# A 32-row block solve on VectorE: the next row finished by one fused operation, the other rows by product and addition in turn, and semaphore waits where drains stood

## The reference, cut to what matters

```python
q = silu(causal_conv(h @ Wq)); k = silu(causal_conv(h @ Wk)); v = silu(causal_conv(h @ Wv))
...
def step(S, inp):                       # one token of one head
    S = S * exp(g)                      # decay
    delta = (v - k @ S) * beta
    S = S + outer(k, delta)
    return S, q @ S
...
o = rms_norm(o) * g_norm_weight
return x + (o * silu(h @ Wg)).reshape(...) @ Wo
```

## Time and profile before

| | |
|---|---|
| device time, median of three runs | 1336.97 us (1332.95 to 1341.53) |
| span of the profiled execution, first to last instruction | 1334.4 us |
| busy share of the span | PE 84%, DVE 58%, PEld 54%, ACT 49%, POOL 25% |
| DMA | 44.83 MB, mean 34 GB/s |
| the three block solves, from the first transpose's start to the last one's end | 545.66 to 574.60, 662.86 to 691.78, 781.13 to 809.80 us |

### The profile page before, as it was taken

How to read it: one execution, slowest core, us unless ns; L and a number is a source line. 1 busy time by engine, 2 the same in 40 slices (tenths; PEclk the granted TensorE clock), 3 DMA queues, 4 the chain that set the end, 5 groups by cost and what they waited for, 6 DMA issues and landing times. The chain is left out here.

```text
span 1334.4 us, 25691 instructions
## 1 busy us (share of the span) xinstructions
PE 1123.0 (84%) x9898; PEld 723.0 (54%) x9899; DVE 775.0 (58%) x1947; ACT 660.2 (49%) x1386; POOL 334.3 (25%) x321
## 2 busy tenths in 40 slices
PE   6998886687989977779769856978899988798998
PEld 3565564354656633357437625856444444475776
DVE  4565557685654587868786785556372465453111
ACT  2565344552542255867696653535756452345342
POOL 1333300134010046545483510230000034700000
PEclk9999897698999976879988985989899988899999
DMA  7000000200000000000000000080286710000000
GB/s 305 1 1 1 2 3 0 97 1 1 3 2 0 1 1 0 0 2 2 1 1 2 1 1 1 2 352 3 48 178 134 153 17 1 2 3 1 1 0 16
DMA packets 18329, 44.83 MB, mean 34 GB/s; under 512 B 4992, under 2 KB 8096, under 8 KB 17568
## 3 DMA queue, kind: packets, MB, share of 16 engines
q1 hardware_dynamic: 18208, 43.20, 11.3%
HBM read 42.41 MB, written 0.79 MB: 32 GB/s over the span
## 5 line engine op out<-in xcount | busy, mean ns | idle before, releaser
L943 ACT ACTIVATE L_xattn_pT<-banks 128x512 f32<-128x512 f32 x128 | 69.0, 598 | 87.8 <-PE banks L821 87.8
L220 POOL TENSOR_TENSOR norm_rstd<-norm_var,norm_power 128x4 f32<-128x4 f32 x24 | 24.4, 1019 | 330.0 <-DVE norm_var L213 330.0
L1004 DVE TENSOR_REDUCE L_xattn_top<-banks 128x4 f32<-128x512 f32 x128 | 79.5, 684 | 35.0 <-PE banks L789 35.0
L1639 DVE TENSOR_TENSOR L_ffn_a<-L_ffn_a,L_ffn_share 128x512 f32<-128x512 f32 x64 | 39.9, 686 | 60.9 <-DMA L_ffn_share<-L_ffn_shares 60.7
L1866 ACT ACTIVATE L_ffn_aT<-banks,L_ffn_shift 128x512 f32<-128x512 f32 x64 | 43.3, 687 | 58.9 <-PE banks L1818 57.3
L1553 PE MATMUL banks<-L_ffn_a,region_a 128*128 128x512 f32 x136 | 67.5, 601 | 5.0 <-DVE L_ffn_a L1639 5.0
L1879 DVE SCALAR_TENSOR_TENSOR x<-banks,L_ffn_combine,x 128x128 f32<-128x128 f32 x64 | 18.0, 344 | 88.7 <-PE banks L1829 88.7
L1544 PE MATMUL banks<-hT,region_a 128*128 128x512 f32 x136 | 69.1, 614 | 0.0
L1829 PEld LDWEIGHTS banks<-region_b,L_ffn_aT 128*128 128x128 f32 x512 | 59.4, 192 | 6.7 <-issue 6.7
L499 ACT ACTIVATE L_attn_p<-banks,L_attn_shift 128x129 f32<-128x129 f32 x128 | 45.4, 369 | 34.3 <-DVE L_attn_shift L552 34.3
L1829 PE MATMUL banks<-region_b,L_ffn_aT 128*128 128x128 f32 x512 | 59.6, 275 | 0.0
(11 more groups left out here) (549 smaller groups left out, 2900.0 us busy)
## 6 DMA issues: line engine op xcount, KB each, us to landing
L_ffn_share<-L_ffn_shares SPq DMA_DIRECT2D x32, 512.0 KB, 10.6
region_b<-in_L_ffn SPq DMA_DIRECT2D x1, 6216.0 KB, 29.9
region_a<-in_L_ffn SPq DMA_DIRECT2D x1, 4416.0 KB, 13.6
region_b<-in_L_attn SPq DMA_DIRECT2D x1, 3150.5 KB, 10.4
region_a<-in_L_ffn SPq DMA_DIRECT2D x1, 3080.5 KB, 16.4
region_b<-in_L_attn SPq DMA_DIRECT2D x1, 1633.5 KB, 8.7
region_b<-in_L_xattn SPq DMA_DIRECT2D x1, 835.0 KB, 7.4
w_tables<-in_tables SPq DMA_DIRECT2D x1, 832.0 KB, 11.7
```

Of the source, the lines that this page charges most:

```text
L943: nc.scalar.activation(pT[:, n % 2, 4 * i:4 * i + 4, :], rows_of(flip[i][:], 4), ACT.Exp, scale=scale).then_inc(exped, 1)
L1004: nc.vector.tensor_reduce(top[:, 32 * i:32 * i + 32:HD], rows_of(score[i][:], 4), X, ALU.max).then_inc(topped, 1)
L1639: nc.vector.tensor_tensor(a[:, k % AHEAD, :], a[:, k % AHEAD, :], share[:, batch % RING, j, :], ALU.mult).then_inc(weighed, 1)
```

## The change

Finished rows now go back into `blocks`, in SBUF, and `solve`, in PSUM, holds only the sums of rows that aren't finished. Step j makes three operations where it made two:

- the product, now for the rows from j+2 on, (30 - j) x j numbers, with both inputs in `blocks`;
- one `scalar_tensor_tensor`, which finishes row j+1: row j of `blocks` times the number at (j+1, j), plus row j+1 of `solve`, written into row j+1 of `blocks` (j numbers);
- the addition of the product to the rows from j+2 on of `solve`.

Products lie in two buffers in turn. The drains between these operations are gone, but for one in step 1 and one at the end; each operation instead waits at a semaphore for the one that it needs, which stands two places earlier in DVE's order. DVE copies only the first half of `blocks` into `solve`, and ACT the second half (`copy_rest`). The ones of the diagonal are set within step 2, in `blocks`. `lower_c` and AT's diagonal blocks are transposed from `blocks` instead of `solve`. Since `joined` lies over `blocks`, both `keep_join` now wait for the `place_upper` that reads the part that they overwrite, and ACT does both `keep_lower` ahead of both `keep_join`.

```diff
-    step_out = from_spare(256)
+    products = from_spare(2 * 256)
...
+            def copy_rest(hg):
+                act.wait_ge(blocks_taken, hg + 1)
+                act.wait_ge(r_ready, B * (hg + 1))
+                nc.scalar.activation(solve[:, NB // 2:NB, :], blocks[:, NB // 2:NB, :], ACT.Copy).then_inc(rest_copied, 1)
...
             def keep_join(hg, half):
                 act.wait_ge(join_made, 2 * hg + half + 1)
+                act.wait_ge(upper_ready, 4 * hg + 2)
...
                 keep_blocks(first + B - 1)
+                copy_rest(hg)
...
                 keep_lower(hg, 0)
+                keep_lower(hg, 1)
                 keep_join(hg, 0)
                 keep_join(hg, 1)
-                keep_lower(hg, 1)
...
                 nc.vector.transpose(blocks[:], blocks_in).then_inc(blocks_taken, 1)
                 dve.drain()
-                nc.vector.tensor_copy(solve, blocks[:])
+                nc.vector.tensor_copy(solve[:, 0:NB // 2, :], blocks[:, 0:NB // 2, :])
+                rows, rests = (NB - 2) * hg, (NB - 3) * hg
+                for j in range(1, NB - 1):
+                    rest = NB - 2 - j
+                    product = products[:, 256 * (j % 2):256 * (j % 2) + rest * j].rearrange("p (i c) -> p i c", c=j)
+                    if j >= 2:
+                        dve.wait_ge(row_done, rows + j - 1)
+                    if rest > 0:
+                        nc.vector.tensor_tensor(product, bc(blocks[:, j + 2:NB, j], 2, j), bc(blocks[:, j, 0:j], 1, rest),
+                                                ALU.mult).then_inc(product_made, 1)
+                    if j == 1:
+                        dve.drain()
+                        dve.wait_ge(rest_copied, hg + 1)
+                    else:
+                        dve.wait_ge(rest_done, rests + j - 1)
+                    nc.vector.scalar_tensor_tensor(blocks[:, j + 1, 0:j], blocks[:, j, 0:j], blocks[:, j + 1, j:j + 1],
+                                                   solve[:, j + 1, 0:j], ALU.mult, ALU.add).then_inc(row_done, 1)
+                    if rest > 0:
+                        dve.wait_ge(product_made, rests + j)
+                        nc.vector.tensor_tensor(solve[:, j + 2:NB, 0:j], solve[:, j + 2:NB, 0:j], product,
+                                                ALU.add).then_inc(rest_done, 1)
+                    if j == 2:
+                        nc.vector.memset(blocks[:].rearrange("p t s -> p (t s)")[:, 0:NB * NB:NB + 1], 1.0)
                 dve.drain()
-                nc.vector.memset(solve.rearrange("p t s -> p (t s)")[:, 0:NB * NB:NB + 1], 1.0)
-                dve.drain()
-                for j in range(1, NB - 1):
-                    rest = NB - 1 - j
-                    product = step_out[:, 0:rest * j].rearrange("p (i c) -> p i c", i=rest)
-                    nc.vector.tensor_tensor(product, bc(blocks[:, j + 1:NB, j], 2, j), bc(solve[:, j, 0:j], 1, rest), ALU.mult)
-                    dve.drain()
-                    nc.vector.tensor_tensor(solve[:, j + 1:NB, 0:j], solve[:, j + 1:NB, 0:j], product, ALU.add)
-                    dve.drain()
                 after(dve, lower_kept, 2 * hg)
-                nc.vector.transpose(lower_c, solve.rearrange("p t s -> p s t")).then_inc(lower_ready, 1)
+                nc.vector.transpose(lower_c, blocks[:].rearrange("p t s -> p s t")).then_inc(lower_ready, 1)

             def place_upper(b):
                 nc.vector.transpose(AT[BLOCKS[b], :, :, BLOCKS[b]].rearrange("p b h t -> p t (b h)"),
-                                    solve[BLOCKS[b], :, :]).then_inc(upper_ready, 1)
+                                    blocks[BLOCKS[b], :, :]).then_inc(upper_ready, 1)

             def keep_join(hg, half):
                 dve.wait_ge(join_made, 2 * hg + half + 1)
+                dve.wait_ge(upper_ready, 4 * hg + 1)
```

More of the change, by code:

```diff
@@ L2907, in delta_rule @@
              "gate_kept", "later_ready", "mcoef_ready", "seg_made", "dec_ready", "scaled", "keys_made", "a_ready", "p_ready",
-             "blocks_act", "blocks_taken", "values_made", "r_ready", "lower_ready", "upper_ready",
+             "blocks_act", "blocks_taken", "rest_copied", "row_done", "product_made", "rest_done", "values_made", "r_ready", "lower_ready", "upper_ready",
              "join_made", "join_kept", "join_kept_too", "lower_kept", "corner_made", "corner_kept", "low_made", "low_kept",
@@ L2915, in delta_rule @@
      gate_kept, later_ready, mcoef_ready, seg_made, dec_ready, scaled, keys_made, a_ready, p_ready,
-     blocks_act, blocks_taken, values_made, r_ready, lower_ready, upper_ready,
+     blocks_act, blocks_taken, rest_copied, row_done, product_made, rest_done, values_made, r_ready, lower_ready, upper_ready,
      join_made, join_kept, join_kept_too, lower_kept, corner_made, corner_kept, low_made, low_kept,
```

## The result

The changed kernel took 1355.24 us (median of four runs, 1345.58 to 1358.21), the kernel before 1339.2 us (four runs, 1332.95 to 1341.53). The ratio is 1.0114, with a 95% interval of 1.0076 to 1.0153: slower by 1.1%. The profiled execution of the changed kernel is the one of 1345.58 us, span 1343.8, its quickest; so differences between the two profiles are read stretch by stretch here, not over the whole span.

What follows compares the result with a forecast made beforehand. The prediction took the solve on DVE to set the end of its stretch in each group. Two groups later by 12.8 and 12.5 us, the third 7.0 sooner: +18.3 on 1337, so 1355 us, range 1345 to 1376.

Steps and rivals of the forecast that it cites:

- The products stand still behind POOL's additions.: Solves of the first two groups: products with both inputs in SBUF wait until POOL's addition, about 2 us, is through.
- One product per POOL operation, 13 in all, and a handover also without a pause.: First solve: products 11 to 23 each enter as a POOL operation ends, also at four pauseless places; transpose 12.8 us later.
- Alone the solve ends 7.0 us sooner.: Solve loop with nothing beside it, as in the third group: 18.7 us instead of 24.85, starting 0.9 us sooner.
- The waits cost nothing.: Semaphore waits between the solve's DVE operations: taken as 0, upper bound 0.11 us for each operation.
- The transposes from SBUF instead of PSUM: 1.25 us in either case, nothing.: Transposes at the end of the solve: reading `blocks` instead of `solve` leaves them at 1.25 us, no cost.
- The rest costs nothing.: `copy_rest`, ACT's new order, squares and taps: nothing; first corner between 0.5 us sooner and 0.6 later behind `lower_ready`.
- The sum.: Whole kernel, three groups: 12.8 + 12.5 - 7.0 = +18.3 us, median 1355 us.
- The rivals.: Products not held: 1329 us, chance 0.08; waits cost as much as drains: 1384, 0.06; POOL waits for products: 1337, 0.06.
- the first: Rival for the first two solves: products aren't held up by POOL, ACT sets the corners; 8 us sooner, 1329 us, chance 0.08.

Runs made afterwards that it cites:

- the waits alone: Kernel before, with semaphore waits in place of the loop's drains, product and addition in turn, no fused row: 1324.25 us, ratio to the kernel before 0.9887.
- the run with the coefficients in PSUM: Changed kernel, with the product's coefficients read from `solve` (PSUM) instead of `blocks` (SBUF): 1328.86 us, ratio to the kernel before 0.9915.
- the second wait: The waits alone, with a second, long satisfied wait on `blocks_taken` ahead of each addition: 1339.58 us (one run).

## Why the prediction was right, point by point

- **The products stand still behind POOL's additions.** Right, and shown from two sides: with one input in PSUM (0.38 us for 1.95) and with POOL's work away (392 ns at most). It is no share of a bandwidth: with POOL's operations cut in halves, the same numbers moved held the products for 0.8 to 1.2 us each, in place of 1.6 to 2.1. L3703 and L2489, which the prediction also reads, have one input in SBUF (1.99 and 0.55 us); the runs here show the hold for products with two. What lies behind the hold no run shows.
- **One product per POOL operation, 13 in all, and a handover also without a pause.** Right: 13 were held. They were numbers 12 to 24, not 11 to 23, since eleven products were under way or done when POOL began, not ten. The transpose started 12.03 and 12.05 us later within its solve (39.72 and 39.73 us against 27.69 and 27.68), for 12.8 and 12.5 predicted. At 554.30 and the three other places without a pause the product did get in.
- **Alone the solve ends 7.0 us sooner.** Right: 20.08 against 27.41 us in the third group, 7.33. The old additions took 197 ns for 30 numbers where the products took 186, which is the prediction's 0.165 us against 0.155; that the PSUM source makes the difference, no run shows.
- **The waits cost nothing.** Right: the additions (L3669) and products have no idle time before them, the fused operations 0.6 us in 90, all of it at step 1 (behind the drain that is left) and step 30 (0.10 us, with no product between it and the addition that it waits for). Elsewhere the products, fused operations and additions start 0.05 to 0.10 us before the end of the product, fused operation or addition ahead. A drain put back costs 0.18 us each.
- **"The transposes from SBUF instead of PSUM: 1.25 us in either case, nothing."** This step failed. The 1.25 us of the earlier trace rows are one transpose that reads SBUF in its order and one that reads PSUM crosswise (neighbouring inputs lie 32 numbers apart). The new one reads SBUF crosswise, which no row of before showed, and takes 1.90 us (579.57 above): 0.65 us in each group, 1.96 in all. It is 1.25 again where it reads PSUM (576.68 above). `place_upper`, which also reads its source elsewhere now, stayed at 1.9 us (1.88 to 1.94 before, 1.89 to 1.90 after). The step had taken a time measured from one source and one order of reading for another.
- **The rest costs nothing.** The first corner starts 4.96 us behind `lower_ready` (586.44 - 581.48), now released by `keep_join` as predicted, against 4.75: within the 0.6 us given. In the other groups it is 4.69 against 4.76 and 4.66.
- **The sum.** 12.03 + 12.05 - 7.33 + 1.96 = +18.7 us, for +18.3 predicted: the hold-up came out 1.2 us smaller than predicted, the third group's gain 0.3 larger, and the transposes added 1.96. The medians differ by 16.0. That 1355.24 lies on the 1355 forecast is luck in part: the difference came out 2.3 us smaller than forecast and the kernel before, with its fourth run, 2.2 us slower than the 1337 that it was added to. In the profile the stage grew by 14.0 us, as the stretch ahead of the first solve was 2.7 us shorter, at a granted clock of 0.83 against 0.77, and the three behind the solves 2.0 us.
- **The rivals.** None came about. The time of the first, 1329 us if products aren't held up, was worked out from ScalarE's bound, and the run in which they are not gave 1328.86. Its corners began 0.3, 2.1 and 6.8 us sooner behind the first transpose's start than those of the kernel before, for the 0.6, 0.6 and 7.0 reckoned.

## What to carry to other kernels

Before an operation on VectorE is rewritten, look where each of its inputs lies and what GpSimd does beside it: with both inputs in SBUF beside GpSimd's additions the solve took 39.7 us, and with one of them taken from a copy in PSUM 19.96. Put semaphore waits in place of drains in a chain of short operations (0.03 to 0.04 us between neighbours here, for 0.08), one wait to an operation (the second cost 0.07), and set an independent operation between writer and reader where there is one (the next then started 0.08 before the end). With the waits alone the ratio is 0.9887, and no version with a fused row is faster than that by more than the runs can tell. When the chain is shorter than the other engines' work beside it (ScalarE in two of three groups here), look next at the order of that work.

## What had not been expected of the hardware

- The transpose of 128 x 1024 numbers at the end of a solve took 1.25 us from PSUM read crosswise, and from SBUF read crosswise 1.90 us in the changed kernel and up to 2.01 us in the run with the coefficients in PSUM.
- On VectorE, of two dependent neighbours in the solve the second started 0.03 to 0.04 us behind the end of the first with one semaphore wait between (the waits alone), 0.08 with a drain (the kernel before), 0.10 to 0.11 with two waits of which one is long satisfied (the second wait); with another operation between writer and reader (the changed kernel) it started 0.08 before the end of that one (547.74 + 0.37 against 548.03).
- Between two POOL operations without a pause, VectorE's held operation still got in (554.95 to 556.67 and 557.04 to 558.80 in the changed kernel, within the three additions from 554.30); three POOL additions that took 6.59 us took 6.72 then.
- The granted clock behind the third solve rose from 0.50 at another time in the kernel with the waits alone, and the stretch behind that solve was 3.7 us shorter, of a stage of 386. The cause is open.
